# Pairing 64-row remainders of two matmul groups on the two halves of the TensorE array, with new per-engine order lists

## The reference

```python
h = silu(einsum('th,ehi->tei', x, gWg) + gbg) * (einsum('th,ehi->tei', x, gWu) + gbu)   # gate * value
out_e = einsum('tei,eih->teh', h, gWd) + gbd                                             # down
moe_out = einsum('te,teh->th', c, out_e)          # c: four routed experts a token, else 0
hs = silu(x @ sWg + sbg) * (x @ sWu + sbu)        # the shared expert, the same form
return moe_out + hs @ sWd + sbd
```

## Time and profile before

| what | value |
|---|---|
| median of 3 runs | 258.57 us (258.42 to 259.27) |
| span of the profiled execution, first to last instruction | 257.6 us |
| mean granted TensorE clock over the span | 0.996 of full |
| TensorE matmuls busy (PE) | 245.2 us, 95% of the span |
| TensorE weight loads busy (PEld) | 222.6 us, 86% |
| VectorE (DVE), ScalarE (ACT), GpSimd (POOL) busy | 191.2, 151.5, 17.1 us |

### The profile page before, as it was taken

One profiled execution on the slowest core, in us unless ns is written; L12 is line 12 of the kernel. 1 busy time (PEld: TensorE's weight loads), 2 busy tenths in 40 slices (PEclk: granted clock), 3 DMA queues, 4 the chain that ended last, 5 costly groups with the idle time before them and its releaser, 6 DMA issues.

```text
span 257.6 us, 4492 instructions
## 1 busy us (share of the span) xinstructions
PE 245.2 (95%) x1508; PEld 222.6 (86%) x1508; DVE 191.2 (74%) x491; ACT 151.5 (59%) x312; POOL 17.1 (7%) x26
## 2 busy tenths in 40 slices
PE   6988879999999998999999999999999999999994
PEld 4866458578588898999999999999999999999993
DVE  4459988999989998999797799887333175853542
ACT  2399798988868998853795971426441432132220
POOL 5100202003101000101100000101000010000000
PEclk9999999999999999999999999999999999999998
DMA  5668563000000342000003520000144000015500
GB/s 154 211 191 286 212 186 119 0 3 0 0 0 6 84 111 57 0 3 0 1 3 121 187 76 4 1 3 0 54 163 158 29 3 0 1 23 109 102 29 26
DMA packets 13015, 17.49 MB, mean 68 GB/s; under 512 B 2336, under 2 KB 11074, under 8 KB 12866
## 3 DMA queue, kind: packets, MB, share of 16 engines
q1 hardware_dynamic: 12722, 17.11, 22.3%
q10 hardware_dynamic: 272, 0.11, 0.2%
HBM read 16.22 MB, written 0.99 MB: 67 GB/s over the span
## 4 chain that ended last, share of the span: by engine, by line
PE 74%; DVE 9%; ACT 9%; issue 3%; DMA 2%; POOL 0%; SPq 0%; DVEq 0%; POOLq 0%; ACTq 0%
PE PG L964 18%; PE PA L984 17%; PE PG L966 11%; PE PF L984 7%; PE PQ L964 4%; PE PQ L966 3%; PE PX L1001 2%; PE PF L1001 2%; ACT norm L417 2%; DMA w_tok<-in_w_tok 2%; PE PF L974 1%; PE PG L1119 1%; PE PG L1118 1%; DVE K L763 1%; PE PF L991 1%
## 5 line engine op out<-in xcount | busy, mean ns | idle before, releaser
L575 ACT ACTIVATE act<-PG,columns 128x222 f32<-128x222 f32 (+3 forms) x56 | 28.4, 507 | 59.0 <-PE PG L966 45.9
L964 PE MATMUL PG<-stack,hi_egu 128*128 128x222 f32 (+1 forms) x288 | 62.2, 324 | 0.0
L913 DVE SCALAR_TENSOR_TENSOR hid<-PG,columns,act 128x222 f32<-128x222 f32 (+1 forms) x52 | 27.3, 524 | 29.3 <-PE PG L966 26.7
L984 PE MATMUL PA<-w_ed,hid 128*124 128x192 f32 (+1 forms) x240 | 46.1, 327 | 0.6 <-DVE hid L922 0.5
L964 PEld LDWEIGHTS PG<-stack,hi_egu 128*128 128x128 f32 x288 | 45.7, 191 | 0.9 <-DVE hid L913 0.4
L966 PE MATMUL PG<-stack,lo_egu 128*128 128x222 f32 (+1 forms) x192 | 42.8, 304 | 0.0
L984 PEld LDWEIGHTS PA<-w_ed,hid 128*124 128x124 f32 (+1 forms) x240 | 38.6, 183 | 1.3 <-issue 1.3
L966 PEld LDWEIGHTS PG<-stack,lo_egu 128*128 128x128 f32 x192 | 31.8, 191 | 0.0
L391 POOL TENSOR_TENSOR rstd<-var,minus_half 112x2 f32<-112x2 f32 (+3 forms) x12 | 13.8, 1146 | 191.7 <-DVE var L657 191.7
L922 DVE TENSOR_TENSOR hid<-hid,gates 128x222 f32<-128x222 f32 (+1 forms) x48 | 21.9, 461 | 1.6 <-DMA gates<-c_rows 0.7
L984 PE MATMUL PF<-w_down,mix_hid 128*124 128x192 f32 (+1 forms) x120 | 22.8, 326 | 0.0
(11 more groups left out here) (248 smaller groups left out, 441.3 us busy)
## 6 DMA issues: line engine op xcount, KB each, us to landing
gates<-in_w_egu SPq DMA_DIRECT2D x6, 512.0 KB, 4.9
gates<-c_rows SPq DMA_DIRECT2D x16, 138.8 KB, 2.9
gates<-c_rows SPq DMA_DIRECT2D x16, 92.5 KB, 2.7
gates<-c_rows SPq DMA_DIRECT2D x16, 83.2 KB, 2.5
w_ed<-in_w_ed SPq DMA_DIRECT2D x1, 1152.0 KB, 6.1
gates<-c_rows SPq DMA_DIRECT2D x16, 55.5 KB, 2.5
gates<-in_w_up SPq DMA_DIRECT2D x2, 384.0 KB, 4.5
pat<-in_patches SPq DMA_DIRECT2D x2, 370.0 KB, 4.3
```

The source lines that it names most:

```text
L575: nc.scalar.activation(act[128 - gate:128, n % 2, 0:G.n], PG[0:gate, gate_bank(n), 0:G.n], ACT.Silu, bias=bias).then_inc(act_silu, 1)
L913: V_.scalar_tensor_tensor(out, PG[part, 1, 0:G.n], bias, act[part, i, 0:G.n], ALU.add, ALU.mult).then_inc(mul_done, 1)
L964: mm(out, w_hi[:, slot, cols], x[:, p, 0:G.n], start=(p == 0), stop=False, skip_group_check=True)
L984: last = mm(tile_out(P, G, t), src[:, G.ts[t]:G.ts[t] + G.tp], w, start=start and t != 1, stop=stop, skip_group_check=True)
```

## The change

For units 2 to 13 the gate, and for units 1 to 12 the value, is cut to its first four matmuls (first_four). The fifth runs with 64 rows: the value of unit n on rows 0 to 63 and the gate of unit n+1 on rows 64 to 127, one right behind the other, at the end of the step of gate n+1. There are twelve such pairs in each group. So that the value's moving operand lies in rows 0 to 63, ScalarE copies the remainder's high part there once a group (beside, step "b" of track Y). The value's end is thus told to VectorE only after the first four matmuls of the next gate. Many waits are put in another order or asked for once, a wait for the stack's buffer moves from before the step to its writing, a constant tile now lies in part of hid, and all three order lists are new.

```diff
+        beside = sb("beside", [64, N], F32R)
...
         def act_experts(act_e, g):
             G = GROUP[g]
+            act_e.wait_ge(act_high[3], at(act_high[3], g, 2))
+            since(act_e, pe_gate, g)
+            nc.scalar.activation(beside[:, 0:G.n], stack(3, g)[64:128, 1, 0:G.n].bitcast(F32), ACT.Copy).then_inc(act_beside, 1)
+            yield "b"
...
+        def first_four(G, out, x, name, cols):
+
+            for p, slot in enumerate((0, 1, 0)):
+                mm(out, hi[name][:, slot, cols], x[:, p, 0:G.n], start=(p == 0), stop=False, skip_group_check=True)
+            mm(out, lo[name][:, 0, cols], x[:, 0, 0:G.n], start=False, stop=False, skip_group_check=True)
+
...
-                from_stack(G, PG[:, gate_bank(n), 0:G.n], stack3[g % 2], name, slice(first_col, first_col + 128)).then_inc(pe_gate, 1)
+                if g == 0 and first_col == 0:
+                    need(pe, name)
+                gate, value = PG[:, gate_bank(n), 0:G.n], PG[:, 1, 0:G.n]
+                if n < 2:
+                    from_stack(G, gate, x, name, slice(first_col, first_col + 128)).then_inc(pe_gate, 1)
+                else:
+                    first_four(G, gate, x, name, slice(first_col, first_col + 128))
+                    if n == 2:
+                        pe.wait_ge(act_beside, at(act_beside, g, 1))
+                    mm(value, left[0], left[1], start=False, stop=True, skip_group_check=True).then_inc(pe_value, 1)
+                    mm(gate, lo[name][64:128, 1, first_col:first_col + 128], x[64:128, 1, 0:G.n],
+                       start=False, stop=True, skip_group_check=True).then_inc(pe_gate, 1)
                 yield f"g{n}"
                 if n == 0:
                     continue
                 pe.wait_ge(mul_done, at(mul_done, g, n))
-                from_stack(G, PG[:, 1, 0:G.n], stack3[g % 2], name, slice(first_col + 128, first_col + 256)).then_inc(pe_value, 1)
+                if n == UNITS - 1:
+                    from_stack(G, value, x, name, slice(first_col + 128, first_col + 256)).then_inc(pe_value, 1)
+                else:
+                    first_four(G, value, x, name, slice(first_col + 128, first_col + 256))
+                    left = lo[name][0:64, 1, first_col + 128:first_col + 256], beside[:, 0:G.n]
                 yield f"v{n}"
...
-    "G3:g9 D3:d7 G3:v9 G3:g10 D3:d8 G3:v10 G3:g11 D3:d9 G3:v11 G3:g12 D3:d10 G3:v12 G3:g13 D3:d11 G3:v13 D3:d12 D3:d13",
+    "G3:g3 D3:d1 D3:d0 G3:v3 G3:g4 D3:d2 G3:v4 G3:g5 D3:d3 G3:v5 G3:g6 D3:d4 G3:v6 G3:g7 D3:d5 G3:v7 G3:g8 D3:d6 G3:v8",
```

More of the change, by code:

```diff
@@ L196, in build @@
         act, hid, hid_s = sb("act", [128, 2, N]), sb("hid", [128, 2, N]), sb("hid_s", [128, N])
+        still = hid[:, 0, 0:256]
         relu, mix_hid = sb("relu", [128, N]), sb("mix_hid", [128, 2, N])
@@ L425, in act_stack @@
             act_e.wait_ge(pe_transposed[n], at(pe_transposed[n], g, k + 1))
+            if n == 3 and k == 0 and g >= 2:
+                act_e.wait_ge(pe_value, at(pe_value, g - 2, UNITS - 1))
             if n < 3:
@@ L640, in moments @@
             stats, mv, var = (small[n][k] for k in ("stats", "mv", "var"))
-            if n == 1:
-                since(v, act_x0, g)
-                since(v, norm_ready[1], g)
             for t in range(G.tiles):
-                if n == 1:
+                if n == 1 and t % 2 == 0:
                     v.wait_ge(tok_out, at(tok_out, g, 2 if G.rounds == 1 else 1 + t // 2))
+                if n == 1 and t == 0:
+                    since(v, act_x0, g)
+                    since(v, norm_ready[1], g)
                 step(V_.bn_stats(stats[0:G.tp, t, :], x[0:G.tp, t, :]))
@@ L772, in dve_front @@
             yield "z"
-            v.wait_ge(act_x0, at(act_x0, g, 1))
             for bank, a, b in G.banks:
                 v.wait_ge(pe_o, at(pe_o, g, bank + 1))
+                if bank == 0:
+                    v.wait_ge(act_x0, at(act_x0, g, 1))
                 V_.tensor_tensor(x1[0:G.tp, a:b, :], x1[0:G.tp, a:b, :], rows_of(o_banks(g)[bank], G, a, b), ALU.add).then_inc(x1_out, 3 - G.rounds)
@@ L987, in transposed @@
         def transposed(pe, G, g, n, k, bank):
-            pe.wait_ge(norm_ready[n], at(norm_ready[n], g, 1))
+            if k == 0:
+                pe.wait_ge(norm_ready[n], at(norm_ready[n], g, 1))
+            if n == 1 and k == 0:
+                pe.wait_ge(tok_out, at(tok_out, g, 2))
+                if g == 0:
+                    pe.wait_ge(consts_in, 16 * 2)
+            if n == 2 and k == 0:
+                pe.wait_ge(x1_ready, at(x1_ready, g, 1))
+                since(pe, stack_ready[3], g)
             for t in range(G.tiles):
@@ L1020, in spin @@
             def spin():
-                mm(PQ[:, 0:256], still[:, 0:128], still[:, :], start=True, stop=True, skip_group_check=True)
+                mm(PQ[:, 0:256], still[:, 0:128], still, start=True, stop=True, skip_group_check=True)
             pe.wait_ge(pool_set, 1)
@@ L1220, in pe_downs @@
                 if n < SCH:
-                    pe.wait_ge(whole_in["sd"], 16)
                     pe.wait_ge(mul_done, at(mul_done, g, n + 1))
+                    if g == 0 and n == DOWNS[0]:
+                        pe.wait_ge(whole_in["sd"], 16)
                     src, w = hid[:, n % 2, :], whole["sd"][:, n, :]
@@ L1227, in pe_downs @@
                 else:
-                    pe.wait_ge(whole_in["ed"], 16)
                     pe.wait_ge(hid_ready, at(hid_ready, g, n - SCH + 1))
+                    if g == 0 and n == SCH:
+                        pe.wait_ge(whole_in["ed"], 16)
                     src, w = hid[:, n % 2, :], whole["ed"][:, n - SCH, :]
```

82 lines of the change are left out of this document (42 added, 40 removed), and 109 rows, old and new, of tables (ACT_ORDER, DVE_ORDER, PE_ORDER).

## The result

The changed kernel takes 268.90 us (median of 4 runs, 268.35 to 269.64), the kernel before 258.92 us beside it (258.42 to 259.42): the ratio is 1.0368, with an interval of 1.0326 to 1.0409. It is slower by 10.0 us, 3.7%. The forecast was 271.1 us, 12.5 us above the 258.57 us that it started from.

The account below looks back on a forecast made before the run. TensorE was taken to bound the kernel: 12.2 us side by side, 17.7 one behind the other, set at 14.0, less 1.5 absorbed, gives +12.5: span 270.1, plus 0.97, 271.1 us. Range 267 to 276 us at 70%.

Parts of the forecast that it names:

- The trip: On TensorE, around each pair: leaving the full array and coming back costs 0.37 us, read from the 33-row matmuls.
- The net price of a pair: On TensorE, side by side: trip less the matmul saved, 0.26 us more with 222 columns, 0.20 us with 370.
- the rival without a price: On TensorE: 64-row pairs cost nothing for the change of mode, so the kernel gets faster, 254.9 us; chance 10%.
- Side by side: A pair's two halves run at the same time on TensorE: +12.2 us in all, against 17.7 one behind the other.
- a third of the way up: Between halves side by side (12.2 us) and one behind the other (17.7 us), the sum was set at 14.0 us.
- The value's bank in group 3: Group 3: the next value waits 0.92 us for VectorE to empty the bank, which sets the pace; group +4.3 us.
- unit of 2.12: Group 3: one unit takes 2.12 us against 1.76, +0.36 us, or +2.9 us for units 5 to 12.
- the waits put in another order ... are worth nothing: Reordered waits ask for the same events and bring no gain while TensorE is full.
- absorbed: TensorE, 76 to 120 us: 1.5 of the 1.8 us idle time takes up part of the added cost.
- The lists: New order lists: counted as zero, giving back at most 3.4 us idle between 35 and 120 us, or losing as much.
- no wait for VectorE in groups 0 to 2: TensorE waits for no product there, since other groups' work or a longer down product, 0.97 us, mostly stands between.
- the rival with new waits: Halves one behind the other, plus 0.2 us wait for products in 24 units of groups 1 and 2: 279.6 us; 7%.

Follow-up runs that it names:

- e2: Kernel before, with the fifth matmul of gates 2 to 13 on rows 64 to 127 alone, no partner, old lists: 274.88 us, ratio 1.0632.
- e3: Changed kernel with both matmuls of each pair on rows 0 to 63: 274.82 us, ratio 1.0614.
- e1: Changed kernel with the two last matmuls of each pair taking all 128 rows, new lists and late value kept: 262.01 us, ratio 1.0126.
- e8: Kernel before the change, with group 1's store issued after half of group 2's broadcasts of c: 259.11 us, ratio 0.9981.
- e4: Changed kernel without pairs: five full matmuls together again, no copy beside, new lists and waits kept: 261.24 us, ratio 1.0095.
- e6: The new lists without pairs, plus group 1's store issued after half of group 2's broadcasts of c: 258.68 us, ratio 0.9958.
- e9: Changed kernel with full-height last matmuls, plus group 1's store issued after half of group 2's broadcasts of c: 259.49 us, ratio 1.0006.
- e5: Changed kernel with the order lists of before, only ScalarE's copy step put in: 285.97 us, ratio 1.1038.
- e7: Changed kernel with group 1's store issued after half of group 2's broadcasts of c: 268.71 us, ratio 1.0356.

## Why the prediction was right, and where its size was off

**The trip: right.** I read 0.37 us for leaving the full array and coming back from the 33-row matmuls. Two steps of 0.11 would make a pair 0.22 us long and it is 0.60: a trip of 0.38 us, and 0.73 - 0.34 = 0.39 with 370 columns. The net price of a pair was put at 0.26 and 0.20 us and is 0.27 and 0.22. e2 shows this trip without any other part of the change. So the rival without a price fell. The Trainium skill, "TensorEngine Tiling (Array Packing)", section Key Properties, says that changing the mode drains the engine; the trace agrees, with the 0.20 to 0.26 us from the last full matmul to the half loads.

**Side by side: right, but not fully believed.** The forecast took a third of the way up to halves that follow one another, because two loads on one loader seemed to be in the way. They begin less than 0.01 us apart, and e3 shows what one behind the other looks like. The Trainium skill, "TensorE: Matmul & The Clock Gate", section "Measured speedup vs the span model", gives about 4 ns a tile; the starts agree, 3 to 4 ns apart in all 48 pairs, but the rule counts no trip, and by it alone the kernel would have become faster. The step that was mis-sized is this third of the way: 14.0 in place of 12.2 us, 1.8 us too much.

**The value's bank in group 3: wrong, it does not set the pace.** The forecast took a loop of 0.92 us and so a unit of 2.12. The loop is 0.81 us in the changed kernel: of the 0.41 from the half load to the product the half load takes about 0.10, the product follows 0.31 behind that, takes 0.45, and the next load begins 0.05 later. In the unit shown it is 0.91 us from the first load to the eighth full matmul, 0.20 to the half loads, 0.30 to the down product's load and 0.61 to the next value's, which took 0.59 before with no wait for the bank: 2.02 us. That is the 1.76 of before and the 0.26 that a pair was to cost net, with at most 0.02 left for the bank; and e3 found no wait there to hide in. Where no trip lengthens TensorE's own part, in e1, the same loop does set the pace, by 0.05 us a unit. In the changed kernel the bank does hold up value 2, which has no down product ahead of it:

```profile
235.94 0.41 PEld L979 LDWEIGHTS PG<-stack,hi_sgu 128*128 128x128 f32 x3 [0.25 <-DVE hid_s L920]
...
237.95 0.41 PEld L979 LDWEIGHTS PG<-stack,hi_egu 128*128 128x128 f32 x3 [0.72 <-DVE hid L920]
...
244.63 0.43 PEld L979 LDWEIGHTS PG<-stack,hi_egu 128*128 128x128 f32 x3
```

The steps that failed are the unit of 2.12 us and, with it, that "the waits put in another order ... are worth nothing": the new order of VectorE's waits made this loop 0.10 us shorter, and with 0.92 us it would, by the forecast's own sum, have set the pace.

```diff
+                if n:
+                    v.wait_ge(pe_value, at(pe_value, g, n))
+                v.wait_ge(act_silu, at(act_silu, g, n + 1))
...
-                v.wait_ge(act_silu, at(act_silu, g, n + 1))
-                if n:
-                    v.wait_ge(pe_value, at(pe_value, g, n))
```

The value comes last of what the product needs. Where its wait stands last in the code (before, e2, e8), the product of a late unit in group 3 begins 0.41 us after the start of the value's last matmul; where it stands first, with the same full matmuls (e1, e4, e6, e9), 0.31 us. The lists are not the cause: e5 has the changed code with the old lists, and its value 13 of group 3, which has no pair, shows 0.31 too. The records show where the 0.10 us lies. Before, most products carry the wait for the down product themselves, and a separate semaphore instruction ahead waits for the silu and the value: for value 12 of group 3 it is recorded from 250.51 to 250.56, and the product starts at 250.60. In the changed code the product carries the wait for the value, and the separate instruction, with the other two waits, is done earlier. No kernel changes this order alone.

**The sum.** Groups 0 to 2 by measured pairs: 12 x 0.27 + 24 x 0.22 = 8.5 us (7.9 forecast). Group 3: eight units of 2.02 - 1.76 = 0.26 us, and from value 1 to value 5 it takes 244.63 - 235.94 = 8.69 us against 7.68, together 3.1 us (4.3 forecast). That makes 11.6 us; the kernel lost 10.0. The difference of 1.6 us is near the 1.5 us that I took as absorbed in TensorE's idle time, but that is not shown by itself. Between 76 and 120 us the idle time did fall from 1.8 to 0.25 us, though it rose by more than a microsecond both ahead of that and behind it. And the first gate of group 0, ahead of every pair, begins here, first before and then after the change:

```profile
74.01 0.46 PEld L964 LDWEIGHTS PG<-stack,hi_sgu 128*128 128x128 f32 x3
...
72.41 0.41 PEld L971 LDWEIGHTS PG<-stack,hi_sgu 128*128 128x128 f32 x3
```

So 1.6 us were won before any pair ran, and behind that gate the profiled execution lost 10.8 us. In the other kernels with the new lists that gate begins between 73.3 and 75.0 us, with the old lists between 73.2 and 74.2; so this looks like scatter, and no run shows it as a gain of the lists. The forecast's +12.5 was 2.5 us too high: 1.8 from the third of the way, 0.6 from the pairs (0.6 too low) and the bank's loop (1.2 too high) together, 0.1 from the remainder. That the errors in pairs and bank partly cancel, and that the remainder fits, is in part luck.

**The lists: zero in the sum, for a reason that I had not seen.** I counted them at nothing. That came out within the scatter, but it hides two things that do not belong together: without pairs the lists cost 2.6 us by the wait for a store (e4 against e6), of which some 1.1 us is still in the changed kernel's trace (e7), and with the old lists the pairs would cost 17 us more (e5). That I counted no wait for VectorE in groups 0 to 2 rested on the new lists: with them TensorE waits for a product twice, 0.9 us in all, and one of the two is in group 2, 0.39 us just behind the wait for the store. e5 shows such waits, 9.2 us, though with pairs that still run side by side; the rival with new waits, 279.6 us, had them one behind the other.

## What to carry to other kernels

Price a switch of the array's tiling by the whole trip, here 0.37 to 0.39 us, against the matmul that it saves, 0.11 or 0.17 us: from these numbers, as an estimate, a trip pays only if it carries four pairs with 222 columns or three with 370. A result that is completed later holds its bank longer, so a change of this kind must put other work between the completion and the next use of the bank (e5), and when lists move, the in-order DMA queue that nobody edited has to be read again. When an instruction waits for several events, which of the waits it carries itself was worth 0.10 us here; that counts only where the loop that holds it sets the pace, and no run here shows what it is worth to the whole kernel.

## What the hardware showed that I had not expected

- Two weight loads of 64 rows on different halves of the array begin 0.003 to 0.004 us apart (48 pairs) and last 0.18 us each, like one alone; on the same half they begin 0.11 us apart (e3).
- Each of the 24 broadcasts of c takes 0.55 us of SyncE's queue (13.30 us in e4), so a store behind them leaves 13 us after the first of them.
- In the kernels that wait for the value first, the product in group 3 begins 0.10 us sooner (0.31 against 0.41 us in seven kernels): the product carries that wait itself, where a separate semaphore instruction of 0.05 us waited for the value before.
